# Second norm of a decoder layer in two PSUM bank pairs, with the first weight tile decoded ahead of the scan

## The chip, the core and the metric

The program runs on one core of one Trainium2 chip. A core has five engines that run their own instruction streams in order and meet at semaphores: PE (TensorE, matmuls and transposes), DVE (VectorE), ACT (ScalarE), POOL (GpSimd) and SP (SyncE, which here only issues DMAs). The metric is the device time of one launch in microseconds; every comparison is of medians on the same chip.

## What is computed

One decoder layer for 4 sequences of 512 tokens, width 512, in float32. In the reference's terms, cut to what matters:

```
x1  = layernorm(x + attention(x))                # 16 heads, 4 kv heads
y   = scan(ctx) * silu(x1)                       # Mamba block, 16 states, 512 channels
x2  = layernorm(x1 + y)                          # "the second norm"
h   = silu(x2 @ gate.T) * (x2 @ up.T)            # gate = lut[gate_idx], 1376 x 512
out = layernorm(x2 + h @ down.T)                 # down = lut[down_idx]
```

The feed-forward weights are not stored as numbers: each is an index from 0 to 15 into a table of 16 values (`lut`), and the kernel has to decode them.

## The kernel before

**Prologue.** SP asks for the weights and inputs (`ip`, the context, `xT`, then `wqkv`). PE runs a list of jobs (`RAMP_JOBS`) in order: the input projection of sequence 0 (`in_proj`, L533), keys and values (`project_kv`, L542), `x_proj` (L556), `delta_mm` (L569), the rest of keys and queries, and transposes. DVE adds the convolution's taps (`earlier_taps`, L1094), then waits for ACT, does the softplus (L1145 to L1155), then the products of queries and keys (`head_products`, L1109) and the first scans.

**Scan.** 64 groups (4 sequences of 16 states) of 4 scans each (`scan`, L1191, on DVE; L1184 and L1188 where DVE also multiplies by C). Each group needs the C row of its state, repeated on all partitions by a DMA (`repeat_c`, L394). POOL multiplies by C (`output_product`, L1442) and issues DMAs that add the group to a sum in DRAM (`y_scratch`, and `y2_scratch` for odd states). The last 8 groups are added by PE in banks 4 to 7 (`state_summed`, L656), and the sum of the others is loaded and added at the end (`rest_summed`, L662).

**Second norm.** The four rows (one for each sequence) are loaded by SP (`load_row`, L432 for x1 and L434 for y). For rows 0 to 2 POOL issues a DMA that adds the odd states' sum to the loaded y (`add_odd_to_row`, L1469). ACT makes the gates (L964). The gating product is made by DVE for row 0 (L1236) and row 3 (L1233), by POOL for rows 1 and 2 (L1518). Then eight halves (`HALVES`, 2 row tiles each) pass through a pipeline: PE adds x1 and transposed y in a bank (`residual`, L693 and L695); DVE takes the statistics (`norm_stats`, L1245, L1248, L1251); POOL the inverse root (`stage2_rstd`, L1525); DVE the shift (L1256); ACT the result (`norm_apply`, L971); PE transposes it (`x2_over`, L705) into the same pair of banks; ACT and DVE split it in a high and a low part (`x2T_hi`, L982, and `x2T_lo`, L1263). Four bank pairs are used in turn.

**Weight decoding.** A tile of 128 gate and 128 up channels is decoded in 8 leaves (7 by ACT, L1001; the last by POOL, L1535), each a choice between two table values by one bit, and 7 selects by DVE (`select`, L1219), after DVE has spread and masked the bits (L1198, L1203). Then ACT rounds it to a high part (`high_part`, L1008), POOL makes the low part (`low_part`, L1540), and PE uses both (`gate_up`, L720). A tile of `down` weights is decoded in the same way at half the size. In what follows a "select" of a half tile is one with 512 columns. In the norm's pipeline, the selects of gate-up tiles 0 (`FIRST`) and 1 (`SECOND`) are written out by hand between the halves. Then `tile(f)` runs for f = 0 to 8: selects of down tile f, `inner(f, 0)`, selects of gate-up tile f + 2 with `inner(f, 1)` and `inner(f, 2)` between them, `inner(f, 3)`. `inner(f, tb)` (L1270) is the product of silu(gate) and up of one token block. It frees a pair of banks, so `gate_up(f + 1)` waits for it block by block.

**Last stage.** `down` (L744), with the residual and the third norm.

## Time and profile before

| what | value |
|---|---|
| median of 3 runs | 991.81 us (991.14 to 993.93) |
| the profiled execution | 990.59 us, of which 988.8 us is its span |
| PE busy | 869.3 us, 88% |
| DVE busy | 765.2 us, 77% |
| ACT busy | 672.4 us, 68% |
| POOL busy | 481.3 us, 49% |

The stages of the profiled execution by its lines: prologue from 0 to 55 us (the first scan), scan to 541.7, second norm to about 618, feed-forward tiles to 855, down stage to the end. A line of the timeline gives start, duration, engine, line of the program, operation, output<-input with sizes, the number of instructions merged, and in square brackets how long the engine had been idle and what it had waited for. float32 matmuls appear as two records each, transposes as one.

### The profile page before, as it was taken

Reading aid. Unit: us, or ns where it says so; the run is one execution under the profiler, and the core shown is the slowest. Engines: PE = TensorE matmul, PEld = TensorE weight load, DVE = VectorE, ACT = ScalarE, POOL = GpSimd, SP = SyncE. Lnnn points to the kernel's source line nnn. Section 1 sums busy time; section 2 is a strip of 40 time slices with the busy share of each in tenths; the row PEclk is TensorE's granted clock in tenths of the full one; section 3 lists DMA queues with packets and bytes.
Section 4 is the critical chain, followed back from the end, with each engine's and each line's share of the span. In section 5 each row is a group of like instructions: output and inputs, shape, how many; then the busy total and the mean of one; then the engine's idle time right before and its main releaser. Section 6 shows DMA issues by size and latency. Waiting matters only on the chain.

```text
span 988.8 us, 11890 instructions
## 1 busy us (share of the span) xinstructions
PE 869.3 (88%) x3824; PEld 626.4 (63%) x3824; DVE 765.2 (77%) x1066; ACT 672.4 (68%) x994; POOL 481.3 (49%) x445
## 2 busy tenths in 40 slices
PE   6879888787878897787989879899999999899997
PEld 3547654465544674456545457787777778688885
DVE  3797899877998879986788666888888888355442
ACT  4698985789956899668696464777777776242321
POOL 0079867799767998669676631221112111001000
PEclk9789777999779797787979988999999999899998
DMA  8167979589996799967999222111111110223221
GB/s 259 39 168 177 209 161 229 117 221 245 210 224 122 204 241 210 224 125 202 208 289 277 83 96 86 46 61 42 42 42 44 62 42 22 75 86 107 86 64 53
DMA packets 49908, 135.99 MB, mean 138 GB/s; under 512 B 5364, under 2 KB 13684, under 8 KB 41156
## 3 DMA queue, kind: packets, MB, share of 16 engines
q0 software_dynamic: 8064, 58.72, 30.9%
q1 hardware_dynamic: 40432, 76.44, 23.1%
q10 hardware_dynamic: 1364, 0.25, 0.2%
q8 instruction: 23, 0.38, 0.1%
q14 instruction: 25, 0.20, 0.1%
HBM read 57.93 MB, written 78.51 MB: 138 GB/s over the span
## 4 chain that ended last, share of the span: by engine, by line
PE 26%; issue 23%; DVE 23%; ACT 19%; POOL 5%; DMA 4%; DVEq 1%; ACTq 0%; POOLq 0%; SPq 0%
DVE state L1191 6%; PE banks L606 5%; ACT decay L893 5%; PE banks L720 5%; ACT scaled L882 5%; PE banks L744 4%; DVE leaf L1219 3%; DVE w_gu L1219 3%; PE banks L644 3%; PE banks L548 3%; DVE conv_in L1094 3%; POOL state L1442 2%; ACT leaf L1001 2%; DMA hT<-y_scratch 2%; DMA y_scratch<-state 1%
## 5 line engine op out<-in xcount | busy, mean ns | idle before, releaser
L1442 POOL TENSOR_TENSOR state<-state,crep 128x512 f32<-128x512 f32 x243 | 334.8, 1603 | 85.9 <-DVE state L1191 79.7
L1191 DVE TENSOR_TENSOR_SCAN state<-decay,banks 128x512 f32<-128x512 f32 x243 | 280.7, 1202 | 54.2 <-PE banks L644 44.6
L720 PE MATMUL banks<-x2T,wgu 128*128 128x512 f32 x1056 | 246.3, 393 | 4.8 <-DVE hT L1270 4.1
L644 PE MATMUL banks<-ident,scaled 128*128 128x128 f32 x1024 | 175.9, 314 | 69.1 <-DVE state L1191 49.7
L720 PEld LDWEIGHTS banks<-x2T,wgu 128*128 128x128 f32 x1056 | 197.9, 189 | 52.1 <-DVE hT L1270 11.3
L644 PEld LDWEIGHTS banks<-ident,scaled 128*128 128x128 f32 x1024 | 136.2, 161 | 143.1 <-DVE state L1191 63.4
L893 ACT ACTIVATE decay<-delta,negA 128x512 f32<-128x512 f32 x256 | 169.9, 722 | 77.6 <-DVE state L1191 69.8
L882 ACT ACTIVATE scaled<-duT,BT 128x512 f32<-128x512 f32 x256 | 163.8, 720 | 0.0
L1001 ACT ACTIVATE leaf<-idx_sb,table,table_gap 128x1024 f32<-128x1024 uint8 (+1 forms) x132 | 129.4, 1022 | 6.8 <-DVE w_down L1219 3.2
L1219 DVE COPY_PREDICATED leaf<-idx_sb,leaf 128x1024 f32<-128x1024 uint8 (+1 forms) x88 | 94.1, 1069 | 7.1 <-issue 6.1
L1534 POOL TENSOR_TENSOR pool_wait_here<-minus_half 128x1 f32<-128x1 f32 x22 | 4.3, 193 | 180.6 <-DVE w_gu L1219 116.2
L744 PE MATMUL banks<-x2T 128*128 128x512 f32 (+1 forms) x264 | 84.2, 402 | 3.5 <-DVE x2T L1379 3.5
L744 PE MATMUL banks<-x2T,wgu 128*128 128x512 f32 (+1 forms) x264 | 81.4, 390 | 0.0
L1574 POOL TENSOR_TENSOR rstd<-vareps,minus_half 128x1 f32<-128x1 f32 x16 | 8.7, 542 | 141.8 <-DVE vareps L1398 141.8
L606 PE MATMUL banks<-wp,attT 128*128 128x512 f32 x128 | 63.7, 645 | 0.0
L744 PEld LDWEIGHTS banks<-x2T 128*128 128x128 f32 (+1 forms) x264 | 51.4, 195 | 15.0 <-issue 3.9
L1455 POOL DMA_DIRECT2D y_scratch<-state x52 | 56.1, 1079 | 3.1 <-DMA y_scratch<-state 3.1
L744 PEld LDWEIGHTS banks<-x2T,wgu 128*128 128x128 f32 (+1 forms) x264 | 49.6, 188 | 10.4
L1082 ACT ACTIVATE leaf<-leaf,shift,rstd 128x512 f32<-128x512 f32 x16 | 13.1, 816 | 62.6 <-DVE shift L1401 62.6
L1219 DVE COPY_PREDICATED w_gu<-idx_sb,leaf 128x1024 f32<-128x1024 uint8 x33 | 53.3, 1614 | 2.7 <-issue 2.7
L548 PE MATMUL banks<-wqkv,xT_sb 128*128 128x512 f32 x96 | 45.2, 617 | 2.5 <-DVE conv_in L1150 2.5
L1094 DVE SCALAR_TENSOR_TENSOR conv_in<-banks,ch,conv_in 128x511 f32<-128x511 f32 (+2 forms) x48 | 35.4, 744 | 12.7 <-ACT conv_in L790 11.5
(140 smaller groups left out, 1155.6 us busy)
## 6 DMA issues: line engine op xcount, KB each, us to landing
y_scratch<-state POOLq DMA_DIRECT2D x52, 1024.0 KB, 8.5
crep<-c_scratch SPq DMA_DIRECT2D x64, 256.0 KB, 5.4
idx_sb<-in_idx SPq DMA_DIRECT2D x11, 512.0 KB, 3.5
xT_sb<-in_xT SPq DMA_DIRECT2D x16, 256.0 KB, 4.8
y_scratch<-u SPq DMA_DIRECT2D x4, 1024.0 KB, 6.1
y_scratch<-state SPq DMA_DIRECT2D x4, 1024.0 KB, 6.3
leaf<-x_scratch SPq DMA_DIRECT2D x16, 256.0 KB, 2.8
out<-leaf SPq DMA_DIRECT2D x16, 256.0 KB, 2.0
```

Source lines behind the costliest of these rows:

```text
L548: last = mm(banks[:, bank, :], xT_sb[:, t, s, :], wqkv[:, t, 0:QT * P], start=t == 0, stop=t == HT - 1)
L606: last = mm(banks[:, bank, :], attT[:, s, t if s else 0, :], wp[:, t, :], start=t == 0, stop=t == QT - 1)
L644: last = nc.tensor.transpose(banks[:, k % NB, lc * LQ:(lc + 1) * LQ], scaled[:, g % SR, lc, et * P:(et + 1) * P], ident[:])
L720: last = mm(banks[:, 2 * tb + w, :], wgu[par][:, w, ws, t * P:(t + 1) * P], x2T[:, tb, xs, t, :], start=t == 0 and n == 0, stop=t == HT - ...
L744: last = mm(banks[:, bank, :], h[0:rows], w[0:rows, f, :], start=f == 0 and n == 0, stop=f == FT - 1 and n == 2)
L882: A(scaled[:, g % SR, lc, :], duT[m % 2][:, lc, :], ACT.Copy, scale=BT[:, m % 2, lc, n:n + 1])\
L893: A(decay[:, k % DR_RING, :], delta[m % 2][:, et, :], ACT.Exp, scale=negA[:, et, n:n + 1])\
L1001: A(buffer(LEAF_ROLE[j], kind, parity), bit_of(0, kind, parity), ACT.Identity, bias=table[:, 2 * j:2 * j + 1], scale=table_gap[:, j:j + 1] ...
L1094: V.scalar_tensor_tensor(conv_in[:, et, back:], banks[:, bank_of(("in", m, et)), 0:L - back], conv_w(et, TAPS - 1 - back), conv_in[:, et, ...
L1191: V.tensor_tensor_scan(state[:, g % GR, et, :], decay[:, k % DR_RING, :], banks[:, k % NB, :], 0.0, ALU.mult, ALU.add).then_inc(scan_ready, 1)
L1219: V.copy_predicated(buffer(kept, kind, parity), bit_of(bit, kind, parity), buffer(other, kind, parity)).then_inc(mux_ready, 1)
L1442: G.tensor_tensor(state[:, g % GR, et, :], state[:, g % GR, et, :], crep[:, g % CR, :], ALU.mult)\
```

## The change

Three parts.

1. **The first tile is decoded in the prologue.** Its indices (512 KB) and the table are loaded by SP, the table ahead of everything and the indices ahead of `wqkv`. DVE spreads and masks the bits between the convolution taps; POOL makes 6 leaves, ACT 2, each in its own buffer (the still empty `state`, `scaled` and `decay`); DVE makes 6 selects ahead of the softplus and 1 behind it. The result is stored to DRAM (`w0_scratch`) and loaded back into `w_gu` after the scan. PE gets 4 matmuls on zeros at the very start, and one job (`kv` 2) moves behind `x_proj`.
2. **The end of the scan.** The table and the indices are no longer loaded ahead of the last C row. Row 3's y goes to `leaf` and waits only for its sum; its x1, the decoded tile and two index tiles are loaded behind it. ACT makes the decays of the last sequence behind other work of the same step. DVE gates all four rows.
3. **The second norm.** PE only transposes y (`y_over`); x1 is added by DVE (`norm_stats`), which writes SBUF and takes the statistics there. The y tiles of the halves use banks 0 and 1 (later 4 and 5), the transposes of x2 banks 2 and 3 (later 6 and 7). `y_over` runs up to three halves ahead, and gate-up tile 0 is worked in quarters between the halves. All selects of `SECOND` come in the last halves and behind them; `inner(0, 0)` and `inner(0, 1)` move from `tile(0)` to there.

```
 prologue, SP:
+                sp.dma_start(first_table, lut.to_broadcast([P, 16])).then_inc(first_lut_in, 16)
                 sp.dma_start(ip[:], ...)
                 load_ctx(0)
                 load_xT(0)
+                sp.dma_start(first_words, idx[0, :, 0:2 * H]).then_inc(first_idx_in, 16)
                 sp.dma_start(wqkv[:], ...)
 PE:
+                for _ in range(WARM):      # WARM = 4
+                    mm(banks[:, 7, :], state[:, 0, 0, 0:P], state[:, 0, 0, :], start=True, stop=True)
-        RAMP_JOBS: in x4, kv 0, kv 1, kv 2, xp, ...
+        RAMP_JOBS: in x4, kv 0, kv 1, xp, kv 2, ...
 DVE:
                 for et in range(ET):
                     earlier_taps(0, et)
+                    if et == 0: (wait for the indices) spread the bits
+                    elif et == 1: mask the bits
+                first_selects(range(6))
                 softplus(0, (0, 1))
                 softplus(0, (2, 3))
+                first_selects((6,))
 ACT, behind silu_u(0) and ahead of keep_kv: two leaves;
      decays(0) and scale_input(0) wait for all seven selects
 SP, last sequence:
-                        if b == S - 1 and n == 11:
+                        if b == S - 1 and n == 13:
                             sp.dma_start(table[:], ...)
-                            load_idx(*FIRST)
-                            load_idx(*SECOND)
+                            sp.wait_ge(y_out, 16)
+                            sp.dma_start(y_last, y_scratch[b]...)
                 sp.wait_ge(decay_ready, UNITS)
                 sp.wait_ge(scaled_ready, S * DS * S)
-                load_row(S - 1)
+                (x1 of row 3) (w_gu <- w0_scratch) load_idx(*SECOND) load_idx("down", 0)
 PE, second norm:
-                residual(0)
-                residual(1)
-                for k in range(6):
-                    residual(k + 2)
-                    x2_over(k)
-                gate_up(0, 0, (0,), first=True)
-                x2_over(6)
-                gate_up(0, 0, (1,), first=True)
-                x2_over(7)
+                y_over(0)
+                rest_summed()
+                y_over(1)
+                y_over(2)
+                for k in range(2 * S):
+                    x2_over(k)
+                    if k + 3 < 2 * S:
+                        y_over(k + 3)
+                    if 3 <= k < 7:
+                        gate_up(0, 0, ((k - 3) // 2,), first=True, halves=((k - 3) % 2,))
                 gate_up(0, 0, (2, 3), first=True)
 DVE, norm_stats(k):
                     for i, lt in enumerate(lts):
-                        V.bn_stats(stats[:, lt, :], banks[:, half_bank(k, i), :])
+                        V.tensor_tensor(x1b[b][:, lt, :], banks[:, y_bank(k, i), :], x1_tile(b, lt), ALU.add)
+                    for i, lt in enumerate(lts):
+                        V.bn_stats(stats[:, lt, :], x1b[b][:, lt, :])
 DVE, order:
-                gap; gate_y(0); bits of FIRST and SECOND; gate_y(3)
-                for k in range(8):
-                    norm_stats(k); selects; norm_shift(k); x2T_lo(k - 2)
-                x2T_lo(6); select 5; x2T_lo(7); select 6
+                gate_y(0) gate_y(1) norm_stats(0) norm_stats(1) norm_shift(0) norm_stats(2) norm_shift(1)
+                x2T_lo(0) gate_y(3) norm_stats(3) second_gap() gate_y(2) norm_shift(2) x2T_lo(1)
+                spread norm_stats(4) mask norm_shift(3) x2T_lo(2)
+                for k in range(5, 8):
+                    norm_stats(k); norm_shift(k - 1); x2T_lo(k - 2); select k - 6 if k > 5
+                norm_shift(7) x2T_lo(6) selects 2 and 3, x2T_lo(7) select 4
+                inner(0, 0) select 5 inner(0, 1) select 6
 ACT, order:
+                gates(0) to gates(3); high_part(0, 0) (waits for the loaded tile); norm_apply(0)
+                for k in range(8):
+                    x2T_hi(k); one leaf of SECOND for k = 2 to 5; norm_apply(k + 1)
+                leaves 4, 5, 6; silus(0, 0); silus(0, 1); high_part(1, 1)
```

## Rows read from the trace of the kernel before

**Rows 1.** Timeline of the loop over tiles, ACT and PE: weight rounding, matmuls.
```profile
663.83 1.06 ACT L1008 ACTIVATE wgu<-w_gu 128x1024 fp32r<-128x1024 f32 x1 [5.00 <-DVE w_gu L1219]
...
674.40 15.92 PE L720 MATMUL banks<-x2T,wgu 128*128 128x512 f32 x67 [0.18 <-DVE hT L1270]
...
686.55 1.06 ACT L1008 ACTIVATE wgu<-w_gu 128x1024 fp32r<-128x1024 f32 x1 [4.98 <-DVE w_gu L1219]
```

**Rows 2.** Timeline of DVE and PE, 616 to 645 us: last select of tile 1.
```profile
616.92 1.39 DVE L1219 COPY_PREDICATED w_gu<-idx_sb,leaf 128x1024 f32<-128x1024 uint8 x1
...
628.92 16.27 PE L720 MATMUL banks<-x2T,wgu 128*128 128x512 f32 x64 [2.55 <-DVE hT L1270]
```

**Rows 3.** Timelines of POOL and PE, 541 to 556 us: what ended late.
```profile
541.08 5.83 POOL L1442 TENSOR_TENSOR state<-state,crep 128x512 f32<-128x512 f32 x3 [6.09 <-DMA crep<-c_scratch]
...
552.18 3.70 PE L662 MATMUL banks<-hT,ident 128*128 128x512 f32 x8 [1.68 <-DMA hT<-y_scratch]
```

**Rows 4.** Chain of work that ended last: start, us, what.
```profile
530.02 22.12 DMA hT<-y_scratch
```

**Rows 5.** DMA queues from 530 to 540 us: packets, MB, share of 16 engines.
```profile
q0 software_dynamic: 238, 1.82, 87.2%
q1 hardware_dynamic: 282, 0.60, 17.2%
```

**Rows 6.** POOL's line L1469, the three odd sums added to rows.
```profile
DMA to landing us min/median/max: 11.2/13.8/14.9
```

**Rows 7.** Timeline of PE, 534 to 600 us: sums, transposes, a start after idling.
```profile
534.55 10.19 PE L656 MATMUL banks<-state,ident 128*128 128x512 f32 x22
...
566.23 1.04 PE L705 MATMUL banks<-ident,rows_in 128*128 128x128 f32 x8
...
595.17 2.07 PE L693 MATMUL banks<-hT,ident 128*128 128x512 f32 x2 [3.44 <-DVE x2T L1263]
```

**Rows 8.** Timeline of DVE and ACT in the second norm: prices of single steps.
```profile
542.39 1.20 DVE L1333 TENSOR_SCALAR table_gap<-table_gap 128x8 f32<-128x8 f32 x1
543.50 2.28 DVE L1236 TENSOR_TENSOR rows_in<-rows_in,gate_in 128x2048 f32<-128x2048 f32 x1
...
568.25 1.28 DVE L1245 BATCH_NORM_STATS2 stats<-banks 128x6 f32<-128x512 f32 x2
...
568.36 1.45 ACT L971 ACTIVATE rows_in<-banks,shift,rstd 128x512 f32<-128x512 f32 x2 [1.46 <-DVE shift L1256]
...
570.65 1.25 ACT L1001 ACTIVATE leaf<-idx_sb,table,table_gap 128x1024 f32<-128x1024 uint8 x1
```

**Rows 9.** DVE's instructions grouped by line and shape: count, busy, mean ns.
```profile
L1170 DVE TENSOR_TENSOR x_sb<-banks,x_sb 128x512 f32<-128x512 f32 x12 | 8.1, 678 | 2.7 <-PE banks L606 2.6
```

**Rows 10.** Prologue: chain, then PE's and DVE's timeline.
```profile
7.31 3.71 PE banks L533 x4
...
16.14 5.42 PE L542 MATMUL banks<-wqkv,xT_sb 128*128 128x256 f32 x24
21.75 3.60 PE L556 MATMUL banks<-u,xp_w 128*48 128x512 f32 x8 [0.19 <-ACT u L798]
26.12 5.41 PE L569 MATMUL banks<-bc_dt,dt_w 17*128 17x512 f32 x8 [0.77 <-ACT bc_dt L816]
...
30.38 1.29 DVE L1145 TENSOR_SCALAR delta<-banks 128x512 f32<-128x512 f32 x2 [9.34 <-ACT conv_in L837]
...
41.62 2.29 DVE L1109 TENSOR_TENSOR prod_a<-banks,kv 128x2048 f32<-128x2048 f32 x1 [1.58 <-PE banks L548]
```

**Rows 11.** DMA issues up to 60 us: size, median us to landing.
```profile
wqkv<-in_wqkvT SPq DMA_DIRECT2D x1, 1536.0 KB, 10.8
```

**Rows 12.** Timeline of DVE and POOL at 620 us: a small select beside POOL's work.
```profile
619.49 2.41 POOL L1540 TENSOR_TENSOR wgu<-w_gu,wgu 128x1024 fp32r<-128x1024 f32 x1
...
620.86 1.67 DVE L1219 COPY_PREDICATED w_down<-idx_sb,leaf 128x512 f32<-128x512 uint8 x1 [2.54 <-issue]
622.42 0.75 DVE L1219 COPY_PREDICATED leaf<-idx_sb,leaf 128x512 f32<-128x512 uint8 x1
```

More of the change, by code:

```diff
@@ L329, in loads_of @@
             if kind == "gate_up":
[L330 to L331 removed]
+                return f
+            return f + 1
         def wide(kind):
@@ L898, in _ @@
                 silu_u(0)
-                for s in range(S - 1):
+                act.wait_ge(first_gap_step, 2)
+                act.wait_ge(first_bits_step, 2)
+                for j in (6, 7):
+                    A(first_leaf(j), first_bit(0), ACT.Identity, bias=first_table[:, 2 * j:2 * j + 1],
+                      scale=first_gap[:, j:j + 1]).then_inc(first_end_ready, 1)
+                for s in range(2):
                     keep_kv(0, s)
@@ L919, in _ @@
                             scale_input(g)
+                        if g < DS * S and more:
                             decays(g)
@@ L931, in _ @@
                             normalized(b)
+                        if g < DS * S and not more:
+                            decays(g)
                         if more:
@@ L1336, in _ @@
+                gate_y(0)
+                gate_y(1)
+                norm_stats(0)
+                norm_stats(1)
+                norm_shift(0)
+                norm_stats(2)
+                norm_shift(1)
+                x2T_lo(0)
+                gate_y(3)
+                norm_stats(3)
+                second_gap()
+                gate_y(2)
+                norm_shift(2)
+                x2T_lo(1)
                 spread_bits(*SECOND)
-                single_bits(*FIRST)
+                norm_stats(4)
@@ L1338, in _ @@
                 single_bits(*SECOND)
-                gate_y(3)
-                MUXES = [(FIRST, (0, 1)), (FIRST, (2, 3)), (FIRST, (4, 5)), (FIRST, (6,)), (SECOND, ()),
-                         (SECOND, (0, 1)), (SECOND, (2, 3)), (SECOND, (4,))]
-                for k in range(2 * S):
+                norm_shift(3)
+                x2T_lo(2)
+                for k in range(5, 2 * S):
                     norm_stats(k)
-                    chunk, steps = MUXES[k]
-                    select(*chunk, steps, then=("down", 0) if chunk == SECOND else None)
-                    norm_shift(k)
-                    if k >= 2:
-                        x2T_lo(k - 2)
+                    norm_shift(k - 1)
+                    x2T_lo(k - 2)
+                    if k > 5:
+                        select(*SECOND, (k - 6,))
@@ L1349, in _ @@
+                norm_shift(7)
                 x2T_lo(6)
+                select(*SECOND, (2, 3), then=("down", 0))
+                x2T_lo(7)
+                select(*SECOND, (4,))
+                inner(0, 0)
                 select(*SECOND, (5,))
-                x2T_lo(7)
+                inner(0, 1)
                 select(*SECOND, (6,))
```

257 lines of the change are left out of this document (154 added, 103 removed).

## Prediction

> **What bounds the kernel now.** I read the loop over tiles first, then what sets its start, then the prologue. In the loop ACT rounds a weight tile each 686.55 - 663.83 = 22.72 us, and each time it has idled 5.0 us for DVE's last select [rows 1]. PE starts a tile's block as DVE's `inner` of the tile before frees a bank pair [rows 1]; that `inner` stands behind the down selects. 24 records of a block take 24 x 0.23 = 5.5 us, a tile 22, less than 22.72. So the reader is to see that in the loop PE follows DVE's decoding by a hair, and that the end of the kernel hangs on one moment: S, the end of the last select of gate-up tile 1, read at 616.92 + 1.39 = 618.3 [rows 2]. PE's own start at 628.92 waits 2.55 us for DVE [rows 2]. What comes after S keeps its length if DVE's list does. An earlier start of PE's first tile is by itself worth nothing.
>
> S in turn hangs on the start of the second norm. POOL's last three products waited 6.09 us for the last C row, and PE then 1.68 us for row 3's y [rows 3], which took 22.12 us from issue to landing [rows 4]. From 530 to 540 us the software queue's adds held 87.2% of the DMA engines [rows 5], and SP's queue moved 0.60 MB in 282 packets of some 2 KB, against 238 packets there [rows 5]: turn about, packet by packet. (The Trainium skill, "DMA: Bandwidth & Descriptors", section "Queues, rings and completion order", says that each DMA engine takes the queues in turn, a packet at a time. The rows agree.)
>
> **The change, part by part.** I first work on before's clock and then shift.
>
> *Start of the norm.* 1 MB of indices no longer stands before the last C row, and x1 of row 3 no longer before its y. In the order of one queue the C row then comes well before 538, so POOL's 6.09 us go and it ends by 540. Next late is PE: from 534.55 it has 13 sums (26 records; 22 took 10.19 us [rows 7]), to about 546.4. Row 3's y, asked for at about 528, is 128 packets of 8 KB; at 24 to 28 packets a us beside the adds that is 5 us, more since they are larger, so I take it landed by 545. Bounds: 535, and 552.1 as now [rows 3]. The odd sums' adds land 11.2 to 14.9 us after their issue [rows 6]; row 1's, the second, now gates DVE, and I take 545 (544 to 549). The decoded tile stands behind x1's small packets; I take 552 to 554, and ACT must have it by about 553.5.
>
> *The chain to S.* `y_over` replaces matmuls of two records by transposes of one: 8 of them take 0.9 us [rows 7], where `residual` for a half took 3.5. Against that DVE adds x1: 0.68 us a tile [rows 9], 0.6 in a run. One `norm_stats` is 2 x 0.6 + 1.28 [rows 8] + 0.5 estimated for its small steps = 3.05 us. The chain: PE 546.4 + y_over(0) 0.9 + rest_summed 3.5 (8 records took 3.70 [rows 3]) + first half of y_over(1) 0.5 = 551.3. From there DVE is full: stats 1 to 4 at 3.05 = 12.3; x2T_lo(0) and (1) 2.6; gate 3 as four tiles 2.5 and gate 2 at 2.2 [rows 8]; second_gap 1.9 (its longer half is 1.20 [rows 8], I take both as they ran); spread and mask 1.7; small steps 0.5. That is 23.7, to 575.0. Then handshakes bound it: ACT's leaf 1.2 and norm_apply 1.4 [rows 8]; x2_over(3) and y_over(6) at the low clock 3.5, for PE idled behind gate 2, and a start after 3.44 us of idling took 1.03 us a record, against 0.46 [rows 3, 7]; a quarter tile 3.2, partly at that clock; x2_over(4), y_over(7) and a quarter 4.5; to x2_over(6) 4.2; it and a quarter 3.6; x2_over(7) and ACT's half 1.5; leaves 4 and 5 at 1.2 each 2.3. Sum 25.4, to 600.4. Last, DVE: four selects at 1.4 [rows 2], two inners at 0.6, x2T_lo(7) 1.2, mask 0.4 = 8.4, S = 608.8. I add 0.7 for landings at the late side of what I took: 609.5. The same hand working of before's order, with before's landings, gives 617.4 where 618.3 is read, so the gain is counted between worked numbers: 617.4 - 609.5 = 7.9 us. Bounds: second_gap at 0.4 us and no late landing, 607.3 (gain 10.1); y at 552.1 as now, 615.9 (gain 1.5).
>
> *Moved work.* DVE's list behind S loses inner(0, 0) and inner(0, 1). One stood where the next leaf was 0.2 us away, so 1.05 us (0.5 to 1.4). In tile 1 PE then waits for inner(0, 2) some 2.5 us and runs a stretch at the low clock, costing 2.2; it is ready at tile 2 within 0.5 us of DVE, and gains 0.9 us a tile on it, so I cost this at nothing; without that slack it would cost 2. Decays behind other work of their step: ACT is two groups ahead, nothing. The store of the decoded tile (SP, behind the C row of group 3) has to end before the 13th scan, at about 78 us; asked for at about 66, nothing, or 3 us if it lands ten late.
>
> *Prologue.* Removed: the first four PE records took 3.71 us at the low clock [rows 10]; behind the zeros they take about 1.8, gain 1.7 to 1.9 (0 if the clock is low again). Added: the table's DMA ahead of all, 0.6. The 512 KB of indices delay `wqkv`, which landed 10.8 us after its issue [rows 11] and let the keys start at 16.14 [rows 10], to about 18.0. PE then ends its in_proj at about 14.8 and idles 3.2 us, close to the 3.44 of [rows 7], so kv 0 and kv 1 (16 records of 0.23 us) run mostly at the low clock, 6 instead of 3.6, to 24.0. x_proj, 3.60 [rows 10], ends at 27.6, then kv 2 1.8, and `delta_mm` starts at 29.4 instead of 26.12 [rows 10]: +3.3. If the clock stays high it is +1.7, set by DVE's bits (0.7 and 0.65) on the tap chain and by kv 2. DVE has idled 9.34 us before its softplus at 30.38 [rows 10]; six selects, 8.2 us, from 21.6, end at about 30, ahead of 33.7. The seventh, 1.4, lies in the 1.58 us that DVE waited for PE at 41.62 [rows 10]. Prologue: +3.0 us, bounds +0.5 and +4.5.
>
> A row speaks against the cover of the selects: a small select took 1.67 us beside POOL's low part, against 0.75 behind it [rows 12], and six POOL leaves of 1.2 us now run beside the taps and the selects. Three of them held off by 1.2 each end the selects at 33.6, just in time. (The Trainium skill, "SBUF — State Buffer", section "SBUF: two separate sides", calls the port pair of DVE and POOL an exclusive lock, the loser fully blocked. By that rule alone, with all six in the way, the selects would end at 37.2.)
>
> **Sum.** On the profiled execution, 990.59: + 3.0 - 7.9 - 1.05 = 984.6. It lies 1.2 under the median, so 985.8.
>
> **Rivals.**
> (a) *The selects take the place of the wait for ACT.* All six POOL leaves hold DVE off: 30 + 7.2 = 37.2, 3.5 later than above, on every chain of the prologue. 985.8 + 3.5 = 989.3: no change. For: [rows 12]. Against: a tap reads PSUM and is no select, and half the leaves run beside taps.
> (b) *PE's queue is held by `rest_summed`, slower.* It now stands ahead of y_over(1). If y lands at L after 546.5, S moves with it one for one: S = L + 63.8. At 552.1 the total is 985.8 + 6.4 = 992.2, no change. It is slower beyond 0.3% from L = 555, at 557 it is 997. For: x1, the tile and indices follow on the same queue, and the landing was 22.12 us [rows 4]. Against: 8 KB packets, and nothing stands ahead of it.
> (c) *The change doesn't reach the end.* If the loop were bound by PE itself, its start would count: tile 1 from 628.92 to about 613, some 12 us, and the time 991.8 + 3.0 - 12 = 983; if by DVE as above, 985.8. If instead the decoded list merely slides until ACT's leaves bind it, nothing but the 1.05 is kept: 991.8 + 3.0 - 1.05 = 993.8. Against the last: ACT idled 5.0 us each tile [rows 1].
> (d) *Faster still.* PE stays at the high clock through the norm (-2), and in the prologue (-1.6): 982.2.
>
> **How the numbers follow.** 0.3%, 3 us, is about what a measurement of this kernel tells from no change. Forecast 985.8 with its own range 982.5 to 988.8: 0.50. (d) and PE-bound (c), 979 to 982.5: 0.17. (a) 0.10 and (b) up to 555, 0.09, no change; the sliding list of (c) 0.03, no change. (b) beyond 555 and prologue and landing late together, slower: 0.11. Faster 0.67, same 0.22, slower 0.11. The range leaves 0.08 out below and 0.11 above: 981 to 994.5.
>
> **What would show it.** The first softplus at 33.4 instead of 30.38; kv 0 at about 18 at half clock. No wait of POOL for the last C row; y landed by 545; y_over(1) at 551 + 3 on the new clock; S at 609.5 + 3.0 = 612.5; PE's tile 2 some 6 us earlier than now; tiles at 22.7 us as before. Wrong if rounding tiles has another period, if `rest_summed` waits, or if the first scan is over 5 us late.

## The result, and the profile after

The changed kernel takes 980.51 us (median, 979.72 to 981.78) against 992.87 (991.14 to 994.53) for the kernel before on the same chip: ratio 0.987, 95% interval 0.9852 to 0.9889. It is 1.3% faster. The forecast was 985.8 with 981.0 as the low end of its range; the measured time lies 5.3 us below the forecast and half a microsecond below the range.

The profiled executions are 990.59 (before) and 979.72 (after), spans 988.8 and 977.9, a difference of 10.9. The views below follow it through the kernel. First the busy time by stage, before and after, each cut at its own landmarks: first scan, last own scan step, first step of the norm, last select of tile 1. Columns: window, its length, busy us of PE, PE's weight load, DVE, ACT and POOL (instructions), granted clock, DMA share, GB/s.

```profile
0.00:55.00 55.00, 44.74 (x138) 24.26 (x139) 32.57 (x44) 29.77 (x50) 0.29 (x5) 0.91 0.42 134
55.00:541.70 486.70, 404.95 (x1862) 269.16 (x1861) 420.03 (x444) 396.11 (x649) 396.18 (x357) 0.85 0.87 205
541.70:557.70 16.00, 12.00 (x29) 4.85 (x28) 10.28 (x12) 8.01 (x8) 13.51 (x7) 0.89 0.54 158
557.70:618.30 60.60, 52.85 (x276) 40.68 (x275) 42.48 (x94) 32.45 (x44) 15.86 (x12) 0.89 0.21 75
```

```profile
0.00:57.10 57.10, 47.12 (x147) 25.20 (x148) 44.42 (x59) 32.08 (x52) 12.52 (x20) 0.94 0.42 139
57.10:541.40 484.30, 394.93 (x1856) 261.82 (x1855) 420.02 (x444) 398.40 (x651) 399.73 (x359) 0.87 0.87 206
541.40:548.70 7.30, 7.30 (x23) 3.52 (x22) 4.55 (x3) 0.00 (x0) 0.00 (x0) 1.00 1.04 224
548.70:609.00 60.30, 45.49 (x225) 36.80 (x224) 52.05 (x107) 32.34 (x44) 11.24 (x11) 0.86 0.27 103
```

The reader is to see the lengths: the prologue is 2.1 us longer, the scan 2.4 shorter, the gap between scan and norm 7.3 instead of 16.0, and the norm itself, down to the last select of tile 1, 60.3 instead of 60.6. The scan's 2.4 us are the last C row too. DVE multiplies by C itself in the last step, and in the kernel before it waited there:

```profile
541.09 0.69 DVE L1188 TENSOR_TENSOR state<-banks,crep 128x512 f32<-128x512 f32 x1 [2.62 <-DMA crep<-c_scratch]
```

From the first scan to the last one, which does not need that row, it is 482.3 us before and 482.4 after. The new norm changed how the engines are used (PE 45.5 us for 52.9, DVE 52.1 for 42.5), and hardly its length. It no longer holds tile 0's selects and has additions and gatings on DVE in their place; no run separates these parts.

The prologue's timeline (PE, then DVE), the lines that answer to [rows 10]:

```profile
7.36 7.11 PE L554 MATMUL banks<-ctx_sb,ip 128*128 128x512 f32 x16 [0.26 <-DMA ctx_sb<-in_ctxT]
17.57 3.69 PE L563 MATMUL banks<-wqkv,xT_sb 128*128 128x256 f32 x16 [3.10 <-DMA wqkv<-in_wqkvT]
...
21.69 2.13 DVE L1325 COPY_PREDICATED state<-scaled,state 128x1024 f32<-128x1024 uint8 x1
...
28.61 1.35 DVE L1325 COPY_PREDICATED state<-scaled,state 128x1024 f32<-128x1024 uint8 x1 [1.25 <-issue]
...
32.60 1.26 DVE L1176 TENSOR_SCALAR delta<-banks 128x512 f32<-128x512 f32 x2
```

Softplus starts at 32.60 (before 30.38), and there is no bracket behind it: DVE came to it straight from its selects. But the selects hold it by little. It also needs ACT's first logarithm, which was ready 1.7 us later than before, at about 32.0 against 30.3 (two merged steps, so the first ends halfway):

```profile
31.37 1.07 ACT L861 ACTIVATE conv_in<-banks 128x512 f32<-128x512 f32 x2
```

So 1.7 of the 2.2 us come by the chain through taps, `x_proj` and `delta_mm`, and the selects add the last 0.5. The first scan starts at 57.14 against 54.99. The keys' product ran at the full clock (16 records in 3.69, granted clock 1.00 from 15 to 22 us), although PE had stood idle for 3.10 us.

The end of the scan and the start of the norm (POOL, PE, DVE, and y's DMA issue), which answer to [rows 3, 4]:

```profile
537.55 3.73 POOL L1524 TENSOR_TENSOR state<-state,crep 128x512 f32<-128x512 f32 x3 [0.26 <-DVE state L1224]
...
536.82 11.32 PE L677 MATMUL banks<-state,ident 128*128 128x512 f32 x26
547.98 1.04 PE L715 MATMUL banks<-ident,rows_in 128*128 128x128 f32 x8
548.85 3.60 PE L683 MATMUL banks<-leaf,ident 128*128 128x512 f32 x8
...
548.72 1.29 DVE L1282 TENSOR_TENSOR rows_in<-banks,rows_in 128x512 f32<-128x512 f32 x2 [1.07 <-PE banks L715]
...
leaf<-y_scratch SPq DMA_DIRECT2D x1, 1024.0 KB, 10.9
```

POOL's 6.09 us of waiting for the last C row are 0.26. PE goes through its sums and y_over(0) into `rest_summed` without a wait, since y, issued at 531.54, landed 10.9 us later, at 542.4. DVE's first step of the norm starts at 548.72; before it was 557.77.

The last stretch (DVE's select 3 and 6 of tile 1, ACT's roundings, PE's tiles 1 and 2), which answers to [rows 2]:

```profile
601.04 1.40 DVE L1252 COPY_PREDICATED leaf<-idx_sb,leaf 128x1024 f32<-128x1024 uint8 x1 [3.42 <-issue]
...
607.60 1.40 DVE L1252 COPY_PREDICATED w_gu<-idx_sb,leaf 128x1024 f32<-128x1024 uint8 x1
...
609.04 1.06 ACT L1046 ACTIVATE wgu<-w_gu 128x1024 fp32r<-128x1024 f32 x1 [5.93 <-DVE w_gu L1252]
630.80 1.06 ACT L1046 ACTIVATE wgu<-w_gu 128x1024 fp32r<-128x1024 f32 x1 [4.22 <-DVE w_gu L1252]
653.55 1.06 ACT L1046 ACTIVATE wgu<-w_gu 128x1024 fp32r<-128x1024 f32 x1 [5.01 <-DVE w_gu L1252]
...
612.67 12.79 PE L743 MATMUL banks<-x2T,wgu 128*128 128x512 f32 x48 [2.94 <-POOL wgu L1629]
629.51 20.72 PE L743 MATMUL banks<-x2T,wgu 128*128 128x512 f32 x83 [4.05 <-DVE hT L1313]
```

S, the end of the last select of tile 1, is 607.60 + 1.40 = 609.0, against 618.3. The next rounding follows after 21.76 us, the one behind it after 22.75, against 22.72 before [rows 1]. PE begins tile 1 at 612.67 instead of 628.92, 16 us earlier, and then waits 4.05 us for DVE.

### The profile page after: what moved, and what is told of

Same layout as the page of the kernel before. It is cut to its first block, busy times and chain, and to the rows that moved or that the text cites. A ratio compares the mean times of both kernels' runs of the same rounds, so it can differ in the third digit from the quotient of the medians.

```text
span 977.9 us, 11750 instructions
## 1 busy us (share of the span) xinstructions
PE 843.4 (86%) x3736; PEld 609.0 (62%) x3736; DVE 779.3 (80%) x1084; ACT 668.1 (68%) x989; POOL 480.1 (49%) x456
## 4 chain that ended last, share of the span: by engine, by line
issue 21%; PE 18%; DVE 15%; ACT 9%; POOL 5%; DMA 1%; DVEq 1%; ACTq 0%; POOLq 0%
PE banks L768 4%; PE banks L627 4%; DVE leaf L1252 3%; PE banks L743 3%; ACT leaf L1036 2%; DVE w_gu L1252 2%; PE banks L677 2%; POOL state L1524 2%; DVE state L1224 2%; PE banks L665 2%; ACT decay L921 2%; ACT scaled L908 2%; DMA y_scratch<-state 1%; DVE idx_sb L1236 1%; DVE w_down L1252 1%
## 5 line engine op out<-in xcount | busy, mean ns | idle before, releaser
L743 PE MATMUL banks<-x2T,wgu 128*128 128x512 f32 x1056 | 250.1, 396 | 10.0 <-DVE hT L1313 5.4
L665 PE MATMUL banks<-ident,scaled 128*128 128x128 f32 x1024 | 171.1, 308 | 77.0 <-DVE state L1224 56.6
L665 PEld LDWEIGHTS banks<-ident,scaled 128*128 128x128 f32 x1024 | 132.4, 157 | 149.6 <-DVE state L1224 65.5
L1036 ACT ACTIVATE leaf<-idx_sb,table,table_gap 128x512 f32<-128x512 uint8 (+1 forms) x126 | 122.5, 1014 | 7.1 <-DVE w_down L1252 3.1
L1252 DVE COPY_PREDICATED leaf<-idx_sb,leaf 128x512 f32<-128x512 uint8 (+1 forms) x84 | 89.0, 1060 | 5.9 <-issue 4.9
L1252 DVE COPY_PREDICATED w_gu<-idx_sb,leaf 128x1024 f32<-128x1024 uint8 x30 | 48.5, 1618 | 0.1
L1046 ACT ACTIVATE wgu<-w_gu 128x1024 fp32r<-128x1024 f32 x11 | 11.7, 1060 | 50.1 <-DVE w_gu L1252 50.1
```

Of the source, the lines that this page charges most:

```text
L665: last = nc.tensor.transpose(banks[:, k % NB, lc * LQ:(lc + 1) * LQ], scaled[:, g % SR, lc, et * P:(et + 1) * P], ident[:])
L743: last = mm(banks[:, 2 * tb + w, :], wgu[par][:, w, ws, t * P:(t + 1) * P], x2T[:, tb, xs, t, :], start=t == 0 and n == 0, stop=t == HT - ...
L1036: A(buffer(LEAF_ROLE[j], kind, parity), bit_of(0, kind, parity), ACT.Identity, bias=table[:, 2 * j:2 * j + 1], scale=table_gap[:, j:j + 1] ...
L1252: V.copy_predicated(buffer(kept, kind, parity), bit_of(bit, kind, parity), buffer(other, kind, parity)).then_inc(mux_ready, 1)
```

## The experiments

Where no other is named, the edit is made to the changed kernel. A ratio is to the kernel before, measured on the same chip together with the experiment. The changed kernel itself was measured together with runs 7, 8, 11 and 12 only (981.2). Elsewhere "above" and "below the changed kernel" are distances to its first median, 980.51, from another chip; of these only those of runs 4 and 5 are clear of the intervals of the ratios, and for the others the traces carry the argument.

**1. A late DVE.** Does the end follow DVE's chain to S?

```
                 inner(0, 1)
+                dve.wait_ge(x2lo_ready, 16)
+                for j in range(4):
+                    V.bn_stats(stats[:, j, :], x2T[:, 0, 0, j, :].bitcast(f32))
                 select(*SECOND, (6,))
```

> The changed kernel with four more statistics instructions on DVE (about 0.65 us each, 2.6 us together, results unused) ahead of the last select of gate-up tile 1. Theory (the end hangs on S, the end of that select, and what follows S keeps its length): S, the rounding of tile 2 (630.8) and the end all move by 2.6 us, time +2.6. Rival (PE's own start sets the end, DVE's list has slack): time +0 to +0.7.

Measured: 983.21 (980.78 to 985.78), ratio 0.9904 (0.9877 to 0.9932), 2.7 above the changed kernel. ACT's roundings all came later and stayed so:

```profile
612.11 1.06 ACT L1046 ACTIVATE wgu<-w_gu 128x1024 fp32r<-128x1024 f32 x1 [8.20 <-DVE w_gu L1252]
633.87 1.06 ACT L1046 ACTIVATE wgu<-w_gu 128x1024 fp32r<-128x1024 f32 x1 [4.25 <-DVE w_gu L1252]
```

That is +3.07 at both, of which 0.85 is a later start of the norm (549.57) and 2.2 the edit (2.6 expected). In the profile the end moved by 1.1 only, because the down product's first group ran 1.6 us faster than in the changed kernel's profile (run 11 below). The median's 2.7 fits, but the intervals of the two ratios overlap (0.9852 to 0.9889 for the changed kernel), so it settles little by itself.

**2. A late PE.** Is PE's earlier start worth anything? A quarter of tile 0 (12 products, 3 us) is made twice.

```
+                gate_up(0, 0, (2,), first=True, halves=(0,))
                 gate_up(0, 0, (2, 3), first=True)
```

> The changed kernel with one quarter of gate-up tile 0 (12 matmuls, 2.7 us) worked twice on PE, ahead of the blocks 2 and 3. Theory: PE waits there anyway (2.94 us for POOL's low part ahead of tile 1 and 4.05 us for inner(0, 2)), so the end moves by 0 to 0.5 us. Rival (PE's start counts): +2.7.

Measured: 980.35 (979.3 to 983.64), ratio 0.9878 (0.9848 to 0.9908).

```profile
612.42 11.17 PE L743 MATMUL banks<-x2T,wgu 128*128 128x512 f32 x48 [1.02 <-POOL wgu L1630]
629.20 21.18 PE L743 MATMUL banks<-x2T,wgu 128*128 128x512 f32 x84 [5.62 <-DVE hT L1314]
```

PE's wait ahead of tile 1 fell from 2.94 to 1.02 and everything behind it stayed where it was. With run 1 this shows that S on DVE sets what follows, and PE's start, within the 2 to 3 us tried here, does not.

**3. The order of the loads alone, in the kernel before.** The table is loaded behind the last C row, and both index tiles behind row 3.

```
-                        if b == S - 1 and n == 11:
+                        if b == S - 1 and n == 13:
                             sp.dma_start(table[:], ...)
-                            load_idx(*FIRST)
-                            load_idx(*SECOND)
...
                 load_row(S - 1)
+                load_idx(*FIRST)
+                load_idx(*SECOND)
```

> The kernel before with nothing changed but the order of SP's loads: the table behind the last C row, both index tiles behind row 3's x1 and y. Theory (the start of the norm was late because the C row and y were, but the indices are needed at once while tile 0 is still decoded in the norm): POOL's 6.1 us wait for the C row goes and the first statistics start 3 to 5 us earlier, but the bits, POOL's gating of row 1 and gate 3 wait for indices that land at about 554, so the time is within -1 and +2 us. Rival (the order of the loads is the gain by itself): -4 to -6.

Measured: 995.0 (993.53 to 997.19), ratio 1.0019 (1.0007 to 1.0032): slightly slower, inside the theory's -1 to +2 us. POOL's wait is gone, and DVE's takes its place (POOL, then DVE):

```profile
536.13 3.71 POOL L1442 TENSOR_TENSOR state<-state,crep 128x512 f32<-128x512 f32 x3 [0.28 <-DVE state L1191]
554.86 4.55 POOL L1518 TENSOR_TENSOR rows_in<-rows_in,gate_in 128x2048 f32<-128x2048 f32 x1 [15.02 <-DVE idx_sb L1203]
...
551.58 0.69 DVE L1198 TENSOR_SCALAR idx_sb<-idx_sb 128x1024 int32<-128x1024 int32 x1 [9.06 <-DMA idx_sb<-in_idx]
...
560.69 5.77 DVE L1219 COPY_PREDICATED w_gu<-idx_sb,leaf 128x1024 f32<-128x1024 uint8 x1
```

The old order needs tile 0's indices at the start of the norm. The theory's first half was a miss: the first statistics began at 557.58, not 3 to 5 us earlier than before's 557.77, since y came late (`rest_summed` waited 3.58 us for it, to 550.30) and gate 3 stood behind the late bits. So in the old order putting off the loads gives nothing, and the prologue's decoding is what lets them be put off. Whether the indices could have been loaded still earlier in the scan, without any decoding in the prologue, is not tested.

**4. The old place of the loads, in the changed kernel.**

```
-                        if b == S - 1 and n == 13:
+                        if b == S - 1 and n == 11:
                             sp.dma_start(table[:], ...)
+                            load_idx(*SECOND)
+                            load_idx("down", 0)
+                        if b == S - 1 and n == 13:
...
-                load_idx(*SECOND)
-                load_idx("down", 0)
```

> The changed kernel with the table and the index tiles (gate-up 1 and down 0, 768 KB) loaded where the kernel before did, ahead of the last C row. Theory: the C row is late again (POOL waits about 4 to 6 us for it), y lands near 549 instead of 542.5, rest_summed holds PE's queue and S moves with it: +3 to +6. Rival (y and the C row had slack): 0 to +1.

Measured: 987.7 (983.38 to 995.08), ratio 0.9941 (0.9913 to 0.9969); in the profiles 6.3 above the changed kernel.

```profile
542.41 7.80 POOL L1525 TENSOR_TENSOR state<-state,crep 128x512 f32<-128x512 f32 x3 [5.65 <-DMA crep<-c_scratch]
...
615.40 1.06 ACT L1047 ACTIVATE wgu<-w_gu 128x1024 fp32r<-128x1024 f32 x1 [5.92 <-DVE w_gu L1253]
```

The wait of [rows 3] is back (5.65 for 6.09), the norm starts at 555.03 and S moves with it by 6.4. PE was held by POOL's last products (1.92 and 2.14 us of waiting); `rest_summed` came behind `y_over(0)` at 555.29 without a wait, so here the C row alone did it; the late y, which the theory had as the cause, held nothing. More than half of the change's gain (6.3 of 10.9 us in the profiles) is in this one place in SP's order.

**5. Row 3's y behind the loads that follow it.**

```
-                            sp.wait_ge(y_out, 16)
-                            sp.dma_start(y_last, ...)
...
                 sp.dma_start(w_gu[:], w0_scratch)
+                sp.wait_ge(y_out, 16)
+                sp.dma_start(y_last, ...)
```

> The changed kernel with the last row's y load issued behind the x1 rows and the tile's weights instead of ahead of them. In the changed kernel y lands at 542.5 us and TensorE reaches its sums at 548.85 us without a wait, so there are 6.3 us to spare. Theory (the gain of 9.3 us in the middle is the start of TensorE's sums, which y's place ahead of the other loads pays for): y lands at 549 to 553 us (the other two 2 to 5 us earlier than now), the sums start 0 to 5 us later than now and the last select of gate-up tile 1 moves with them one for one; expected +2.5 us in all, 983.0. Rival (y's order among these loads is without effect, as the three landings come from what the software queue leaves them and from the order of waits behind them): 980.5 within 0.7 us.

Measured: 988.25 (986.47 to 990.95), ratio 0.995 (0.993 to 0.9969): 7.7 above the changed kernel where 2.5 was expected. The mechanism was as expected, the landing was not: y was issued at 535.57 instead of 531.54, took 20.7 us instead of 10.9 and landed at 556.3, outside the 549 to 553 expected.

```profile
556.28 6.01 PE L683 MATMUL banks<-leaf,ident 128*128 128x512 f32 x8 [4.76 <-DMA leaf<-y_scratch]
...
562.83 0.69 DVE L1282 TENSOR_TENSOR rows_in<-banks,rows_in 128x512 f32<-128x512 f32 x1 [8.71 <-PE banks L715]
```

`rest_summed` holds PE's queue, y_over(1) behind it, and DVE stands 8.71 us. S came to 619.0: the prediction's rival (b), S = L + 63.8, gives 620.1 for this landing. (Its own terms give less. `rest_summed` can start at 547.3 there and S is 608.8, so S = L + 61.5, or 62.2 with the 0.7 added for late landings; run 5 has 62.7.) So that rival was a real one, and the issue of y ahead of the small packets is what kept it off.

**6. No decoding in the prologue.**

```
-                first_selects(range(6))
                 softplus(0, (0, 1))
                 softplus(0, (2, 3))
-                first_selects((6,))
```
and likewise without the leaves, the two word steps, their loads and waits.

> The changed kernel without the decode of its first tile: its two word steps, eight leaves, seven selects and their table and index loads are gone, and the tile's weights are raw index words (that part of the output is not the reference's). Everything behind it is kept, the store and the load of the tile too. Theory (the prologue's decode costs 2.2 us because the six selects end at 32.6 us and hold softplus, and everything behind it is moved one for one): the first softplus step at 30.0 to 30.9, first scan at 54.5 to 55.2 in place of 57.14, and the end 2.0 to 2.6 us earlier, so 978.2. Rival (the late wqkv and the delta matmuls behind it hold softplus in any case, and the selects are hidden): first scan at 56.5 or later and a total within 0.7 us of the changed kernel's 980.5.

Measured: 977.87 (977.1 to 981.84), ratio 0.9857 (0.9818 to 0.9897); 2.6 less than the changed kernel, in the median and in the profile. The intervals of the two ratios overlap, but the traces show the 2.6 at the first scan.

```profile
16.20 3.69 PE L560 MATMUL banks<-wqkv,xT_sb 128*128 128x256 f32 x16 [1.56 <-DMA wqkv<-in_wqkvT]
...
29.93 1.29 DVE L1164 TENSOR_SCALAR delta<-banks 128x512 f32<-128x512 f32 x2 [10.41 <-ACT conv_in L858]
...
54.53 2.32 DVE L1212 TENSOR_TENSOR_SCAN state<-decay,banks 128x512 f32<-128x512 f32 x2
```

The first scan is at 54.53 for 57.14. The prologue's decoding costs 2.6 us. Most of it is not the selects: here DVE's taps ended at 19.3 instead of 21.5, as there was no wait for indices (1.01 us) and no bits (0.69 and 0.68) among them; `x_proj`, which needs them by way of ACT's `u`, started at 20.23 instead of 22.36, and the first logarithm was ready 2.1 us earlier. The selects are the remaining 0.5. Against the kernel before (54.99) the rest of the new prologue, the zeros' early matmuls and `kv` 2 behind `x_proj` together, gives back 0.5.

**7. TensorE busy while it waits for `wqkv`.**

```
                     if s == 0:
+                        if c == 0:
+                            for _ in range(6):
+                                mm(banks[:, 7, :], ip[:, 0, 0:P], ip[:, 0, :], start=True, stop=True)
                         pe.wait_ge(xT_in, 64 * c + 64)
```

> The changed kernel with six products of in_proj's size and no use, 2.7 us, on TensorE in the 3.1 us in which it waits for wqkv in the prologue. Theory (it is the idle time that lets the clock fall): idle time ahead of the k and v product 0.3 to 0.6 us, the product at 3.6 to 3.8 us, softplus at 32.4 to 32.7, first scan at 56.4 to 57.2 us and never at 57.8; the median falls by 0.3 to 1.0 us against the changed kernel beside it, and its spread by 1 us. Rival (the clock falls for what came before, not for the idle time): first scan at 57.7 or later in the profile, and no change of the median.

Measured: 984.21 (982.96 to 987.06), ratio 0.9914 (0.9894 to 0.9934), 3.0 above the changed kernel beside it (the intervals just overlap), where 0.3 to 1.0 below was expected. I had sized the six products at 2.7 us; each is two records, and they took 5.31, so the keys started 1.9 us late:

```profile
14.38 5.31 PE L562 MATMUL banks<-ip 128*128 128x512 f32 x12
19.52 3.62 PE L566 MATMUL banks<-wqkv,xT_sb 128*128 128x256 f32 x16
```

The keys' product ran at the full clock behind the filler here and in run 12 (3.62 both times), which fits the theory but is only two executions. With the keys 1.9 us later softplus started at 32.73 for 32.60. PE's chain has less room than that seems to say: of the 1.9 us it lost 1.1 in the wait it had had for ACT's `u` (22.36 in the changed kernel), `delta_mm` came 0.74 later, and ACT's first logarithm was ready at about 32.7, as late as the selects. In run 12, with the same filler and the selects done earlier, softplus waited for it:

```profile
32.71 1.29 DVE L1184 TENSOR_SCALAR delta<-banks 128x512 f32<-128x512 f32 x2 [0.45 <-ACT conv_in L867]
```

Of the 3 us, first scan to first norm step took 493.5 us in the profile for 491.6 in the changed kernel's. PE's rows show where:

```profile
517.45 0.63 PE L668 MATMUL banks<-ident,scaled 128*128 128x128 f32 x4 [2.42 <-ACT scaled L911]
517.91 1.72 PE L680 MATMUL banks<-state,ident 128*128 128x512 f32 x2
```

From this restart PE works without a pause to the first transposes of the norm. Behind it the granted clock was 0.50, the lower of its two levels, from 519 to 521 us, and a pair of sums took up to 1.72 us instead of 1.02; in the changed kernel's profile it was 1.00 there, behind 1.91 us of idling at 516.77. Restart to `y_over(0)` took 32.77 us for 31.21, which is 1.56 of the 1.9. Whether the filler brought this about or chance did is open: runs 9 and 10, without a filler, have the same 32.77.

**8. The changed kernel again,** beside runs 7, 11 and 12.

> The changed kernel once more, with nothing edited, beside the three that follow. Theory (the same program has two prologues: behind TensorE's 3.1 us without work ahead of its k and v product the granted clock stays high in some executions, with that product at 3.7 us, and falls in others, with it at 6.6, the first scan coming 1.2 us later): the single times lie over 2 us or more, 979.5 to 983, median 980.5 to 981.5. Rival (the clock there is a matter of the edits made, not of chance): the first scan is at 57.1 us as in the first profile, and the times lie within 1.5 us.

Measured: 981.2 (979.12 to 985.75), ratio 0.9888 (0.9866 to 0.991). The profile's first scan is at 57.15. The first scan is where the rival had it; the single times spread over 6.6 us, so the theory's spread holds, but this profile doesn't show its cause. The eight profiles that have the changed kernel's own prologue do (this one, the first, and runs 1, 2, 4, 5, 9 and 11): behind 3.1 us of idling the 16 records took 3.69 us in three, 5.38 in three, and 6.58 and 6.72 in two. Here is run 1's:

```profile
17.66 6.58 PE L563 MATMUL banks<-wqkv,xT_sb 128*128 128x256 f32 x16 [3.15 <-DMA wqkv<-in_wqkvT]
...
33.83 1.29 DVE L1176 TENSOR_SCALAR delta<-banks 128x512 f32<-128x512 f32 x2 [1.04 <-ACT conv_in L861]
```

Up to 5.38 softplus hardly moves (32.5 to 32.65 in all six), and with the two slow ones it is 1.2 to 1.3 us later, behind ACT. In run 5 the fall came later, at the queries (4.75 us for 3.60), and put the first scan at 58.34 all the same.

**9. ACT's leaves 4 and 5 of tile 1 ahead of the last two high copies,** to shorten DVE's wait of 3.42 us at 601.04.

```
                 for k in range(2 * S):
+                    if k == 7:
+                        leaves(*SECOND, (4, 5))
                     x2T_hi(k)
...
-                leaves(*SECOND, (4, 5, 6))
+                leaves(*SECOND, (6,))
```

> The changed kernel with ScalarE's leaves 4 and 5 of gate-up tile 1 ahead of the last two high copies of the transposed rows instead of behind them. In the changed kernel VectorE stands idle for 3.42 us ahead of select 3 at 601.04 us, which waits for leaf 5. Theory (VectorE's chain to the end of the last select sets everything behind it): the idle time falls to 1.1 to 1.5 us, the last select ends at 606.6 to 607.0 in place of 609.0, and the total falls by 2.1 us to 978.4. Rival (the high copies, now 2.3 us later, hold the low copies and TensorE's gate-up of tile 0, whose products the two inner steps ahead of the last select wait for): gain of 0 to 0.7 us.

Measured: 979.36 (978.25 to 983.07), ratio 0.9862 (0.9831 to 0.9893).

```profile
603.29 1.40 DVE L1254 COPY_PREDICATED leaf<-idx_sb,leaf 128x1024 f32<-128x1024 uint8 x1 [1.25 <-issue]
...
609.85 1.39 DVE L1254 COPY_PREDICATED w_gu<-idx_sb,leaf 128x1024 f32<-128x1024 uint8 x1
```

The wait shrank by 2.17 as expected. But this execution's norm started at 551.85, 3.1 later than the changed kernel's (1.2 from the prologue, 1.9 from the scan, of which 1.56 is the low clock shown in run 7), and PE's granted clock in it was 0.80 for 0.86; from its start to S it took 59.4 us for 60.3, so 0.9 of the 2.1 arrived. The gain by the median, 1.2 us, is inside the interval.

**10. The same, and in the prologue the select of ACT's leaves one place earlier.**

```
-                first_selects(range(6))
+                first_selects((0, 1, 2, 4, 3, 5))      # select 4 waits for ACT's two leaves only
```

> The changed kernel with both: ScalarE's leaves 4 and 5 of gate-up tile 1 ahead of the last two high copies, and in the prologue the select of the two ScalarE leaves one place earlier, so that it fills VectorE's idle 1.25 us at 27.4 us. Theory: beside the 2.1 us of the first edit the six prologue selects end at 31.3 instead of 32.6, softplus starts at 31.9 to 32.0 (then ScalarE's first logarithm holds it) instead of 32.60, first scan at 56.5 instead of 57.14; the total falls by 2.7 us to 977.8. Rival for the second edit (VectorE's select beside GpSimd's leaf only stretches that leaf by what it fills): no more than the first edit alone gives.

Measured: 981.17 (977.87 to 987.01), ratio 0.9881 (0.9842 to 0.9921). That is 0.7 above the changed kernel where 2.7 below was expected, and no difference by the intervals. The prologue's POOL and DVE:

```profile
27.36 2.27 POOL L1580 TENSOR_SCALAR state<-scaled,decay 128x1024 f32<-128x1024 uint8 x1
...
29.67 1.35 DVE L1328 COPY_PREDICATED state<-scaled,state 128x1024 f32<-128x1024 uint8 x1 [1.08 <-issue]
```

The rival was right for this edit. The select, at 27.27, filled DVE's pause, and POOL's last leaf, 1.20 us when DVE stood idle, took 2.27: the next select came 1.06 later than before, and softplus only 0.25 earlier (32.35). ACT's first logarithm was not ready before about 32.3 here either.

**11. TensorE busy while it waits ahead of the down product.**

```
+                pe.wait_ge(h_ready, FT * 4 - 2)
+                for _ in range(24):
+                    nc.tensor.transpose(banks[:, 3, 0:P], ident[:], ident[:])
                 pe.wait_ge(h_ready, FT * 4)
```

> The changed kernel with 24 transposes of the identity, 3.1 us and without use, on TensorE in the 3.49 us in which it waits ahead of the down product's first group. The first 132 products of this group took 30.2 to 33.1 us in the profiles so far, where 132 at the 0.227 us of the full clock are 30.0. Theory (they start at the low clock behind the idle time, and what differs from run to run is how long it stays low): these 132 take 29.9 to 30.4 us, and the total falls by 1.5 to 2.5 us against the changed kernel beside it. Rival (this group is bound by VectorE and ScalarE making its operands, not by the clock): 31 us or more, and a total within 0.5 us.

Measured: 979.56 (978.23 to 983.05), ratio 0.9874 (0.9852 to 0.9896), 1.6 below the changed kernel beside it, within the two intervals. The changed kernel's profile, then this one's:

```profile
848.74 31.77 PE L768 MATMUL banks<-x2T 128*128 128x512 f32 x132 [3.49 <-DVE x2T L1461]
```

```profile
845.17 2.78 PE L775 MATMUL banks<-ident 128*128 128x128 f32 x24
848.82 30.20 PE L768 MATMUL banks<-x2T 128*128 128x512 f32 x132 [0.87 <-DVE x2T L1464]
```

The group starts at the same time and is 1.57 us shorter, and the span is 1.5 shorter, 976.4. Behind 3.49 us of idling these 132 records took 30.2 to 33.1 us in the other profiles (32.89 in the kernel before), and only one of them, run 1's, had the 30.2 without the transposes.

**12. All four edits.**

> The changed kernel with four edits together: leaves 4 and 5 of gate-up tile 1 ahead of the last two high copies, the prologue's select of ScalarE's leaves one place earlier, six idle products ahead of the k and v product, and 24 idle transposes ahead of the down product. Theory (VectorE's chain to the end of the last select, and the clock at two places): 2.1 for the first (its idle time fell from 3.42 to 1.25 us when it was run alone), 0.6 for the second, 0.3 to 1.0 for the third, 1.5 to 2.5 for the fourth: 4.5 to 6 us below the changed kernel beside it, 975 to 976. Rival (each gain of the clock is given back by another wait): 2 us below at most.

Measured: 979.48 (976.91 to 980.57), ratio 0.9861 (0.9841 to 0.9882), 1.7 below the changed kernel beside it, 2.2 in the profiles. That is the rival's size, not the 4.5 to 6 expected: the down group has its 1.6 (30.21 us), the leaves gave 1.4 from the norm's start to S (58.9 us for 60.2) of 2.1, and the two edits in the prologue nothing, since softplus waited for ACT's logarithm (32.71). It is the fastest version by its lowest time; the medians and intervals don't settle that it beats the changed kernel.

## Where the prediction was right, and which step failed

**What bounds the kernel: right.** What follows hangs on S. The rounding periods kept their 22.7, run 1 moved S and the roundings behind it together, run 2 took away most of PE's wait and changed nothing.

**Where the gain comes from: right in place.** The 9.3 us by which S is earlier are the norm's earlier start (9.05) and nothing else worth naming. It rests on two conditions, the last C row and y in time; run 4 takes back the first and loses 6.3 in the profile, run 5 the second and loses 7.7 in the median. Run 3 shows that moving the loads gives nothing while tile 0 is still decoded in the norm.

**What failed is the size of the gain at S, "617.4 - 609.5 = 7.9 us".** It measured 11.45, beyond even the bound of 10.1 that the prediction set for it, and with the prologue's +3.0, which measured +2.15, it puts the forecast 4.9 us too high in the profiled execution (984.6 worked out, 979.72 read), and 5.3 in the median. By the steps:

- *S, 3.55 us.* On before's clock (less the 2.15 of the prologue) S came to 606.85, a gain of 11.45 against 7.9. DVE's second `norm_stats`, the start of the chain, began at 550.85 (553.00 read) for the 551.3 worked out: 0.45. The stretch in which DVE is full took 22.3 us for 23.7: 1.4. The handshakes took 25.7 for 25.4, which takes 0.3 back, and the last selects and inners 8.0 for 8.4: 0.4. The allowance of 0.7 for late landings wasn't needed: y landed at 542.4 for the 545 taken. And 0.9 was given away by counting the gain from 617.4, a hand working of before's order that the prediction doesn't show, instead of the 618.3 read.

  Inside the full stretch two terms missed by much, in opposite directions:

```profile
565.42 0.16 DVE L1395 TENSOR_TENSOR table_gap<-table 128x8 f32<-128x8 f32 x1
565.61 0.20 DVE L1397 TENSOR_SCALAR table_gap<-table_gap 128x8 f32<-128x8 f32 x1
...
567.92 2.30 DVE L1297 SCALAR_TENSOR_TENSOR shift<-meanvar,rstd 128x2 f32<-128x2 f32 x1
```

  `second_gap`, taken at 1.9, took 0.36. The price in [rows 8] was that of a step beside POOL's products, which the new order no longer has there; in run 3 the same two steps took 0.16 and 0.17. But the small steps, taken at 0.5 in all, took 2.6, as one `norm_shift` stood beside POOL's low part (566.25 to 570.21) and took 2.30 where the others take 0.15. That gave back more than `second_gap` had won, 2.1 against 1.6 us. The 1.4 comes from smaller terms: a `norm_stats` took 2.80 where 3.05 was estimated, four times (1.1), spread and mask 0.5 less, x2T_lo and gate 3 together 0.3 less.
- *The prologue, 0.85 us.* +3.0 was worked out, +2.15 read. Two steps failed. First, the central sum had the clock low behind PE's 3.2 us of idling, with softplus at 33.4 for it; in the profiled execution it stayed high, and then the prediction's own "+1.7" is what ACT's logarithm shows (32.0 against 30.3). The clock behaved both ways: in other executions of the same prologue it fell, and in three of the eight the first scan came 1.1 to 1.2 us later, near the +3.0 (run 8). Second, "six selects end at about 30, ahead of 33.7": they took from 21.69 to 32.6 and are what softplus waits for last, by 0.5. Two took 2.13 and 2.12 instead of 1.37, and DVE paused 1.25 for POOL's held leaf. This is rival (a)'s mechanism in a smaller size: 2.6 late instead of 7.2, where the slack was 3.7 if the clock fell and 2.1 if it stayed high. Four of the six leaves were over by 22.6, beside taps that kept their 0.76 us, and only two met selects. (By the Trainium skill's "SBUF — State Buffer", section "SBUF: two separate sides", applied to all six leaves, the selects would have ended at 37.2. That section has the pair taken by a DVE step in a two-port mode or with two SBUF inputs. The trace agrees: the selects, with two, stretched to 2.13 beside a leaf, and the taps, which read PSUM and one SBUF tile, did not.)
- *The inners: right.* The first period behind S is 21.76 for 22.75, a gain of 0.99 where 1.05 was taken. PE was ready at tile 2 in time.
- *Behind that, 0.6 us,* which the prediction held equal. The tiles took 0.6 longer, the down stage 1.2 less, as its first group ran faster: 31.77 for 32.89 (run 11).

**The median.** The profiled execution was taken as 1.2 below the median, and it was 0.8. The changed kernel's own medians on two chips are 980.51 and 981.2.

**The range** held too little below. The lower end rested on two cases, high clock and a PE-bound loop, and none in which several small prices, all taken on the careful side, were lower together. That is what happened: no single term makes the miss, and 0.45 + 1.4 - 0.3 + 0.4 + 0.7 + 0.9 make the 3.55 at S.

The time from first scan to the norm's first step was 491.1 to 494.5 us in profiles that have the same code there. The low clock behind PE's last pause in the scan is 1.56 of it, in three profiles (runs 7, 9 and 10). What stays open is why PE's restart behind that pause came 459.2 to 461.0 us after the first scan.

## What to carry to other kernels

A stage that is rebuilt may gain little by its new order and most by what the new order no longer needs at its start: ask first which loads can now wait, and what is then late next. Price a small step by a row in which no neighbour holds it up, or by the neighbours that it will have, since the same step took 0.20 and 1.20 us, and another 0.15 and 2.30. And work taken ahead into an engine's idle time is hidden only if its helpers don't stretch one another, here 8.2 us of selects needed 10.9, and if its small first steps don't stand on the chain: here bits and a wait for indices among the taps delayed it by 2.1 us.

## What the runs showed of the hardware

- Whether the granted clock falls behind an idle time of TensorE of 3.1 us isn't fixed: 16 equal records behind it took 3.69, 5.38 or up to 6.72 us in eight executions of the same code, and 132 records behind 3.49 us took 30.2 to 33.1. With transposes that do nothing useful in the pause they took 30.20 and 30.21. At the end of the scan it was 0.50 behind pauses of 2.10, 2.10 and 2.42 us in three executions (32.77 us to the norm's first transposes) and 1.00 behind 1.91 us (31.21).
- DVE and POOL hold each other up in both directions. A select of 1.37 us took 2.13 and one of 1.4 took 5.77 (run 3, beside POOL's gating product), a POOL leaf of 1.20 took 2.27 to 2.31, and a step on 128x2 elements took 2.30 for 0.16, beside POOL's low part.
- The same megabyte in 8 KB packets landed in 10.9 us when it was issued ahead of the small packets of its queue and in 20.7 behind 1.25 MB of them.
